# The first normalisation of chunks 2 and 3 on GpSimd, and a new order of work

## The reference

```
n   = ln(layernorm(x)) * g + b                       # the "first normalisation"
W1  = gelu(n @ h1_w1 + h1_b1) @ h1_w2 + h1_b2        # W2 alike with h2_*
t   = tril(W1 @ W2^T) @ n                            # per sequence of 256 tokens
t   = ln(gelu(t)) * g + b
x1  = layernorm(x) + t
o   = layernorm(x) + gelu(ln(x1)*g+b @ fm_w1 + fm_b1) @ fm_w2 + fm_b2
x   = x + layernorm(o)
y   = layernorm(x)
h   = silu(y @ w1 * s1) * (y @ w2 * s2)              # 128 -> 512
h   = gelu(h @ h1w * s);  h = gelu(h @ h2w * s)      # 512 -> 512, twice
out = x + layernorm(h @ w3 * s3)
```

## Time and profile before

| quantity | value |
|---|---|
| median of 3 runs | 375.56 us |
| profiled execution, its own time | 375.44 us |
| its span in the profile | 373.6 us |
| mean granted TensorE clock | 0.993 |
| executed instructions | 6151 |

### The profile page before, as it was taken

The page is one execution under the profiler, slowest core; times in us unless marked ns, Lnnn a source line. Parts: engine busy times, 40 slices in busy tenths (PEclk is TensorE's granted clock), DMA queues, the critical chain, the costliest instruction groups (busy, mean ns, idle before and its releaser), DMA issues.

```text
span 373.6 us, 6151 instructions
## 1 busy us (share of the span) xinstructions
PE 358.8 (96%) x1848; PEld 294.3 (79%) x1848; DVE 334.5 (90%) x999; ACT 302.2 (81%) x541; POOL 116.8 (31%) x186
## 2 busy tenths in 40 slices
...
DMA packets 8405, 9.10 MB, mean 24 GB/s; under 512 B 561, under 2 KB 6194, under 8 KB 8370
## 3 DMA queue, kind: packets, MB, share of 16 engines
...
q10 hardware_dynamic: 544, 0.26, 0.2%
...
## 4 chain that ended last, share of the span: by engine, by line
PE 72%; DVE 15%; issue 4%; ACT 4%; DMA 2%; POOL 2%; SPq 1%; DVEq 0%; ACTq 0%; POOLq 0%
PE bank L1208 8%; PE bank L1206 8%; PE bank L1222 6%; PE bank L1223 6%; PE bank L1106 5%; PE bank L1103 5%; PE bank L1104 5%; PE bank L1091 4%; PE bank L1087 4%; PE bank L1088 4%; PE bank L1188 4%; PE bank L1191 4%; PE bank L1130 3%; PE bank L1029 3%; PE bank L1117 2%
## 5 line engine op out<-in xcount | busy, mean ns | idle before, releaser
L679 DVE TENSOR_TENSOR ffn_gate_lo<-bank,ffn_gate_hi 128x512 fp32r<-128x512 f32 (+1 forms) x72 | 43.8, 624 | 6.9 <-ACT bank L550 5.4
L478 ACT ACTIVATE h_hidden_hi<-bank,cols 128x512 fp32r<-128x512 f32 x64 | 43.2, 708 | 7.7 <-PE bank L1091 7.5
L679 DVE TENSOR_TENSOR h_hidden_lo<-bank,h_hidden_hi 128x512 fp32r<-128x512 f32 x64 | 42.3, 678 | 3.4 <-ACT bank L483 3.3
L550 ACT ACTIVATE bank<-bank,cols 128x512 f32<-128x512 f32 (+1 forms) x72 | 43.7, 632 | 0.6
L483 ACT ACTIVATE bank<-bank,cols 128x512 f32<-128x512 f32 x64 | 41.8, 684 | 0.3
L1206 PE MATMUL bank<-ffn_gate_hi,ffn_w_hi 128*128 128x512 f32 (+1 forms) x108 | 40.5, 382 | 0.0
L1208 PE MATMUL bank<-ffn_gate_lo,ffn_w_hi 128*128 128x512 f32 (+1 forms) x108 | 39.4, 372 | 0.2 <-DVE ffn_gate_lo L679 0.2
L337 POOL TENSOR_SCALAR ln_f_ve<-ln_f_mv 128x4 f32<-128x4 f32 x7 | 1.6, 228 | 97.6 <-DVE ln_f_mv L669 97.6
L679 DVE TENSOR_TENSOR ffn_h_lo<-bank,ffn_h_hi 128x512 fp32r<-128x512 f32 (+1 forms) x36 | 21.8, 624 | 10.2 <-ACT bank L550 10.2
L544 ACT ACTIVATE ffn_h_hi<-bank,cols 128x512 fp32r<-128x512 f32 (+1 forms) x36 | 22.5, 652 | 10.3 <-PE bank L1208 6.2
L544 ACT ACTIVATE ffn_gate_hi<-bank,cols 128x512 fp32r<-128x512 f32 (+1 forms) x36 | 22.7, 660 | 6.5 <-PE bank L1208 4.0
...
## 6 DMA issues: line engine op xcount, KB each, us to landing
...
```

Source lines behind the costliest of these rows:

```text
L478: nc.scalar.activation(dst, bank(f"{L}u{j}", c)[:, :], ACT.Gelu, bias=bias_of(L, j)).then_inc(*hi[L].done(c, j))
L550: nc.scalar.activation(u, u, ACT.Gelu, scale=cols[:, C_HS[L] + j:C_HS[L] + j + 1]).then_inc(*act2[L].done(c, j))
L679: return nc.vector.tensor_tensor(dst, whole, high.bitcast(f32), ALU.subtract)
```

## The change

The first normalisation of chunks 2 and 3 goes from VectorE (n_first and n_second, 8 instructions of 128 x 128 a chunk) to GpSimd, in four instructions of 128 x 512 a chunk: subtract the mean, times g, times the scale, plus b. The other six chunks keep VectorE's form. The waits that named n_first or n_second now name whichever engine did the chunk. The lists of all engines but SyncE, and TURNS, are ordered anew; the largest differences lie between chunks 1 and 4, small swaps in the later ones. The list ahead of TensorE's branch grows by 16 calls (until up_mm("fm", 3, 0)), taken from the list behind it.

```diff
+        n_pool = steps("n_pool", 4)
...
+        ON_POOL = (2, 3)
+        def turn(c):
+            return ON_POOL.index(c) if c in ON_POOL else c - sum(k < c for k in ON_POOL)
+        def n_centred(c):
+            return n_pool.at(turn(c), 0) if c in ON_POOL else n_v.at(turn(c))
+        def n_done(c, t=T - 1):
+            return n_pool.at(turn(c), 3) if c in ON_POOL else n_v_ready.at(turn(c), t)
...
                 if c:
-                    pool.wait_ge(*n_v_ready.at(c - 1, T - 1))
+                    pool.wait_ge(*n_done(c - 1))
...
+            def n_centre(c):
+                pool.wait_ge(*x_stats.at(c, 1))
+                pool.wait_ge(*nT.at(c - 1))
+                pool.wait_ge(*n_lo.at(c - 1))
+                mean = mv("x", c)[:, :, 0:1].broadcast_to([P, T, D])
+                nc.gpsimd.tensor_tensor(NF[:, :, :], xc(c), mean, ALU.subtract).then_inc(*n_pool.done(turn(c), 0))
+            def n_gain(c):
+                pool.wait_ge(*n_pool.at(turn(c), 0))
+                pool.wait_ge(*rows_ready.at(0))
+                nc.gpsimd.tensor_tensor(NF[:, :, :], NF[:, :, :], row(R_G), ALU.mult).then_inc(*n_pool.done(turn(c), 1))
+            def n_scale(c):
+                pool.wait_ge(*n_pool.at(turn(c), 1))
+                pool.wait_ge(*x_scale.at(c, 1))
+                nc.gpsimd.tensor_tensor(NF[:, :, :], NF[:, :, :], per_token(x_s), ALU.mult).then_inc(*n_pool.done(turn(c), 2))
+            def n_shift(c):
+                pool.wait_ge(*n_pool.at(turn(c), 2))
+                nc.gpsimd.tensor_tensor(NF[:, :, :], NF[:, :, :], row(R_B), ALU.add).then_inc(*n_pool.done(turn(c), 3))
...
-            x_s_(0); x_r(0); n_low(0); xr_scale(0); x_s_(1); x_r(1); xr_b(0); x_s_(2); n_low(1); t_r(0); x_s_(3); x1_r(0)
+            x_s_(0); x_r(0); n_low(0); xr_scale(0); x_s_(1); x_r(1); xr_b(0); x_s_(2); n_low(1); n_centre(2); t_r(0); n_gain(2)
+            n_scale(2); n_shift(2); x_s_(3); x1_r(0); n_low(2); n_centre(3); t_r(1); n_gain(3); n_scale(3); n_shift(3); x_s_(4)
...
-            t_st(0); up_lo("h2", 0, 1); up_lo("h2", 1, 1); t_ag(0); n_first(2); up_lo("h2", 2, 1); up_lo("h2", 3, 1)
-            down_lo("h1", 1); n_second(2); down_lo("h2", 1); lo_raise(); nT_low(2); score_mask(0, 1); score_mask(1, 1)
+            t_st(0); up_lo("h2", 0, 1); up_lo("h2", 1, 1); t_ag(0); x_st(4); up_lo("h2", 2, 1); up_lo("h2", 3, 1); x_ag(4)
+            down_lo("h1", 1); t_gain(0); down_lo("h2", 1); x1_sum(0); score_mask(0, 1); x1_st(0); score_mask(1, 1)
+            score_lo(0, 1); nT_low(2); lo_raise(); score_lo(1, 1); x1_ag(0); x_st(5); up_lo("h1", 0, 2); m_norm(0); t_st(1)
...
-            n_first(3); up_lo("h2", 2, 2); n_second(3); up_lo("fm", 0, 0); t_gain(1); up_lo("fm", 1, 0); up_lo("fm", 2, 0)
+            up_lo("h2", 1, 2); up_lo("h2", 2, 2); up_lo("fm", 0, 0); up_lo("fm", 1, 0); up_lo("fm", 2, 0); up_lo("fm", 3, 0)
+            nT_low(3); branch(0); o_st(0); up_lo("h2", 3, 2); down_lo("h1", 2); up_lo("h1", 0, 3); x_ag(5); o_ag(0)
...
                 for t in range(T):
-                    pe.wait_ge(*n_v_ready.at(c, t))
+                    pe.wait_ge(*n_done(c, t))
                     last = nc.tensor.transpose(bank("nT", c)[:, t * P:(t + 1) * P], NF[:, t, :], ident[:, :])
...
-            down_mm("h2", 3, 1); lo_sum(4); lo_sum(5); lo_count(); n_transpose(2); scores(0, 1); scores(1, 1)
+            down_mm("h2", 3, 1); lo_sum(4); lo_sum(5); lo_count(); scores(0, 1); scores(1, 1); n_transpose(2); up_mm("h1", 0, 2)
+            up_mm("h1", 1, 2); t_product(1); up_mm("h1", 2, 2); up_mm("h1", 3, 2); m_transpose(0); down_mm("h1", 0, 2)
+            up_mm("h2", 0, 2); up_mm("h2", 1, 2); up_mm("h2", 2, 2); down_mm("h1", 1, 2); up_mm("fm", 0, 0); up_mm("fm", 1, 0)
+            up_mm("h2", 3, 2); up_mm("fm", 2, 0); up_mm("fm", 3, 0)
             pe.wait_ge(*lo_flagged.at(0))
             any_lo = pe.value_load(lo_flag[0:1, 0:1].bitcast(i32))
```

More of the change, by code:

```diff
@@ L750, in n_second @@
                     nc.vector.scalar_tensor_tensor(NF[:, t, :], NF[:, t, :], x_s[:, t:t + 1], bc[:, R_B, :],
[L751 removed]
+                                                   ALU.mult, ALU.add).then_inc(*n_v_ready.done(turn(c), t))
             def nT_low(c):
```

213 lines of the change are left out of this document (103 added, 110 removed), and 40 rows, old and new, of the table TURNS.

## The result

| | before | after |
|---|---|---|
| median of 7 runs, us | 375.89 | 378.29 (377.35 to 379.15) |
| ratio, 95% interval | | 1.0056 [1.0031, 1.008] |
| profiled execution / its span, us | 375.44 / 373.6 | 377.35 / 375.6 |

What follows compares the result with a forecast made beforehand. VectorE was taken to set TensorE's pace between 43 and 104 us, the stage changed. +1.6 - 0.3 - 0.6 - 0.15 - 0.25 = +0.3 us on 375.44 gave 375.7 us, range 373.7 to 377.0.

Steps and rivals of the forecast that it cites:

- GpSimd in time: Chunk 2's NF done at about 44.6 us, TensorE asking at about 45.5: 0.9 us to spare.
- First place, +1.6: From 43.08 us to the end of chunk 2's first up product: over at 47.95 instead of 46.36, +1.6 us.
- To o_transpose(0), -0.3: From 46.36 to 66.27 us of before: TensorE waits only once, 0.3 us at 59.4; gain -0.3 us.
- To n_transpose(4), -0.6: The 37.4 us up to 103.68 of before: 2.25 us of waits plus 0.3 small ones; -0.6 us, arriving about 104.4.
- I add nothing: Contention beside GpSimd's new stretches (38.3 to 44.6, 53 to 59.5 us) counted as zero; up to 0.8 us if each overlapped.
- the slower rival: First place not paid back; VectorE 0.7 us later at 66 us turns -0.6 into +0.6: 377.0 us, chance 0.21.
- The rest, -0.4: After n_transpose(4): -0.15 us to y_transpose(1), then -0.25 to 343 us; last chunks' swaps and the branch 0.
- the two small gains of 0.15 and 0.25: 0.15 us by the walk to y_transpose(1); 0.25 to 343 us, as late arrival finds short waits partly over.
- the 1 us given as a sign: Forecast wrong altogether if TensorE's idle time from 104 to 343 us is over 1 us.
- VectorE busy 330.4: Forecast of VectorE's total busy time in the changed kernel: 330.4 us.
- one of its two marks: Signs of being slower: n_transpose(4) after 105.2 us; nT_low(3) starting after 66.8 us.
- The faster rival: VectorE's freed time is used, since all six waits (3.6 us) end with VectorE: 373.7 us, chance 0.34.

Runs made afterwards that it cites:

- h1: c3 with GpSimd writing chunks 2 and 3 to a buffer of its own, n_transpose(2) ahead of the scores, nT_low(2) and x_st(5) moved: 375.56 us.
- c3: The changed kernel with both pairs apart: n_low(3) held until y_norm(0) is over, n_second(4) ahead of branch(1): 376.94 us.
- c2: The changed kernel with only VectorE's n_second(4) put ahead of branch(1): 377.78 us.
- d4: The kernel before with chunks 2 and 3 normalised on GpSimd, no list reordered: 377.06 us.
- d2: The kernel before with only chunk 3's normalisation on GpSimd, no list reordered: 375.13 us, in another series 374.63.
- d1: c3 with chunk 2's normalisation back on VectorE and the first place in before's order, GpSimd keeping chunk 3: 379.44 us.
- g2: c3 with chunk 3's normalisation back on VectorE, chunk 2 alone on GpSimd: 376.69 us.
- g4: d2 with the low parts around 73 to 76 us reordered on GpSimd and VectorE: 376.93 us.
- g5: The kernel before with the same reordering as g4, nothing new on GpSimd: 376.51 us.

## Why the prediction was wrong, point by point

- **GpSimd in time, VectorE's list up to 48 us: right.** NF(2) was done at 43.89 (42.62 + 1.27), or 44.6 by before's start, as forecast.
- **First place, +1.6: right**, +1.68 by the lag. h1 gives the reason the text only implied: with NF in time, and the order that this allows, all but 0.15 of it goes.
- **To o_transpose(0), -0.3: right** (1.38 less 1.68). VectorE idled for 4.9 us (0.7 later) between 57 and 66, where I had 4 or so; two of the rows:

```profile
60.49 1.29 DVE L716 TENSOR_TENSOR fm_hidden_lo<-bank,fm_hidden_hi 128x512 fp32r<-128x512 f32 x2 [1.02 <-ACT bank L520]
...
65.39 0.69 DVE L716 TENSOR_TENSOR aT_lo<-bank,aT_hi 128x512 fp32r<-128x512 f32 x1 [2.34 <-ACT aT_hi L494]
```

- **To n_transpose(4), -0.6: wrong, it was +0.6** (105.7 - 103.68 - 1.38). This is the step that failed, and in it the sentence "I add nothing" on contention. I looked for VectorE's two-input instructions only beside GpSimd's *new* stretches, 38 to 60 us, and weighed them there rightly. The pairs that cost stand at 84 and 103 us, between four instructions that the change didn't touch but whose order it changed. I read the order for what each step waits for, not for what then runs at the same time on the port that the two engines share. I had the price in hand, 0.75 us; the text says that contention is in the slower rival, but that rival's sum has no term for it. The Trainium skill (SBUF — State Buffer, "Who interferes with whom") says that besides an instruction with two SBUF inputs one in a two-port mode, such as a tensor_scalar can be, contends too, and that in that mode whichever engine issues first has the shared ports for its whole instruction, while the other blocks. The trace agrees as to the length: the one slow instruction of y_norm(0), a tensor_scalar from SBUF to SBUF, took 1.45 us for 0.34 and ended 0.08 behind n_low(3). Which of the two was first the rows don't settle, since they start 0.07 apart. My text had weighed only half of that rule. Without the pairs, in c3, this step comes to -0.2 (n_transpose(4) at 104.15 + 0.7): so the first pair is 0.85 of the miss of 1.2, and the rest is the walk itself: it had 2.55 us of waits up to n_transpose(4), where c3 has about 3.4 by the lag from 54 on, and before 3.6, where I had read 3.1.
- **The rest, -0.4: wrong, +0.6.** It is the wait at 106.20. It belongs to the second pair, which lies just ahead of it: c2, without that pair, has a lag of 7.81 at 93 where after has 8.44. In c3 this step is +0.1, so 0.5 of its miss is that the two small gains of 0.15 and 0.25 did not come. From there to the end of the steady stage TensorE idled 0.53 us, under the 1 us given as a sign, and the difference stays at 2.6: the order of the last chunks and the place of the branch cost nothing, as said.
- **VectorE busy 330.4: wrong by 2.5 us**, and this was the first number to show where to look: 1.9 are the two pairs.
- **The rivals.** The slower one named the sum (377.0) nearest to the result, and one of its two marks was met (n_transpose(4) after 105.2). The other was not: nT_low(3) began at 65.39 + 0.7 = 66.1, not after 66.8, so VectorE was in time at 66 and was made late at 84. The mechanism was another, though the rival has a part: with the pairs apart c3 still loses 2.1 us between 66 and 93, where before loses 0.5. The two lag tables show something that had not been foreseen: from 54 to 93 of the work every kernel in them without the pairs loses nearly the same, 3.4 to 3.6 us, whatever its order (before 3.63, d4 3.61, d2 3.64, c3 3.47, d1 3.45, g2 3.45, h1 3.37), and after 4.92. What an order earns by 66 it has given back by 93. The faster rival's ground, that all six old waits end with VectorE, was no evidence: d2 and d4, with less work on VectorE, lose as much between 54 and 66 of the work as before does (3.1 us), and g4 and g5 only moved the waits.

So the 2.4 us are 1.4 of two pairs and about 1.0 of NF's lateness, with the order built around it, that is not paid back. Not settled is h1's remaining lag at 340 (0.24 over before). Its last step on NF(2) meets a low part of the weights (1.79 us for 1.21), but at 34 to 36 us of the span, ahead of the place from which the lag is counted; so that cannot be the 0.24, and no other cause was tried.
